# Early passes, new orders at both ends, and multiplications of ones, in a four-layer graph kernel on one core

## The chip, the core and the metric

The kernel runs on one core of a Trainium2 chip. The metric is the device time of one execution in microseconds (us). A core has TensorE (PE, matmuls into the accumulation memory PSUM), VectorE (DVE), ScalarE (ACT), GpSimd (POOL) and SyncE (SP, which here issues all DMAs). Each runs its own instructions in order and waits on semaphores.

## The reference

x is 128 graphs of 128 nodes with 256 features, adj 128 matrices of 128 x 128. Four graph layers follow each other, each with a residual and a layer norm:

```
x = _layernorm(x + _L0_gnn_ref(x, adj, ...))   # hypergraph conv 256->512, relu, norm, conv 512->256, + x
x = _layernorm(x + _L1_gnn_ref(x, adj, W))     # relu([x, (adj @ x) / deg] @ W.T)
x = _layernorm(x + _L2_gnn_ref(x, adj, ...))   # three times adj @ (x @ W) + b, relu behind the first two
x = _layernorm(x + _L3_gnn_ref(x, adj, ker))   # relu((adj @ x) @ ker) * (row of x is not all zero)
```

In layer 0 the incidence matrix is H = (adj != 0), used as D^-1 H B^-1 H^T.

## The kernel before

**Work.** Two graphs at a time make a pair; there are 64 pairs. For each pair TensorE works through 18 groups of matmuls, named by stage: G, Tr, Gx, R (in two halves), P (two halves and the sums of squares, psum<-ones,sq), GP for layer 0; xT, XAB, AXB for layer 1; Ax2, H1, H1W, H2, H2W, AP3 for layer 2; Ax3, TK for layer 3. Most products are made from a high and a low part of each operand (X_hi rounded to fp32r, X_lo = X - X_hi): hi x hi, hi x lo, lo x hi. `product` issues these three for each term, behind a wait for the high and the low part of the data. Gx, Ax2, H2 and Ax3 are plain fp32 products with the state as the stationary side, and psum<-A_f,x is both Ax2 and Ax3.

**Between the groups.** ScalarE takes a result out of PSUM and rounds it (`high_...`, `round_...`), VectorE or GpSimd makes the low part (`low_...`). A norm (n1 to n4) goes: sum, `stats`, `mean_var` (together `moments`) on VectorE, `root` on ScalarE, `invert` and `shift` on VectorE, and the scaling on ScalarE (`make_x2`, `make_x3`, `make_x4`; in the profile ACT x L961). `make_x3` gives the x that Ax3 multiplies.

**Order.** Each engine has `fill()`, `body(n)` for n from 7 to 61, and `drain()`, written out as lists of calls. In `body` pairs n to n-5 are in flight at once, one stage each. Which PSUM bank (0 to 7) a stage writes is in BANK, and for the pairs of fill and drain in BANK_OF; a wait on TensorE keeps a stage from writing a bank that is still read:

```
def bank(stage, pair):
    return BANK_OF.get((stage, pair), BANK[stage])
def make_x3(p):
    if begun(p - 1):
        act.wait_ge(pe_did["Ax3"], upto(p - 1))
        act.wait_ge(n4.summed, upto(p - 1))
        act.wait_ge(x3_nz, upto(p - 1))
    apply(n3, p, x3)
```

`upto(p)` is the semaphore's value when pair p has passed. `copy_GT(p)` and `round_GT(p)` read the transposes of Tr(p) from their bank, bank 0 in the loop. `wide_var`, `root_h` and `make_p` make the norm inside layer 0; `root_h` is ACT h_std in the profile. In the fill `w2_columns` (psum<-w2g,ones) and `betaW_rows` (psum<-n_s,beta_b) are two sums over the weights.

Of the kernel before, what the change touches and what calls it, by code (L numbers as in the profile page):

```python
# [16 lines left out]
BANK = dict(R0=1, R1=0, Ax2=0, Tr=0, GP=4, H1=1, Gx=1, XAB=2, AXB=2, TK=2, H2=3, xT=4, P=4,  # L17
# [30 lines left out]
def build(nc, x, adjT, w1T, w2T, wab, v1, v2, v3, wk, columns, rows, eye, out):  # L48
# [5 lines left out]
    with ExitStack() as ctx:  # L54
# [23 lines left out]
        eps_c, wait_pad = sb("eps_c", [1]), sb("wait_pad", [1])  # L78
# [46 lines left out]
        class Norm:  # L125
            def __init__(self, name, sums=True, lag=0, moments=None):
                if sums:
                    self.s = sb(f"{name}_s", [2, D])
                self.st, self.lag = sb(f"{name}_st", [2, 6]), lag
# [160 lines left out]
        def _(sp):  # L290
# [37 lines left out]
            def fill():  # L328
                load_at(0)
                sp.dma_start(columns_s[:], columns).then_inc(columns_loaded, 16)  # L330
                load_at(1)
                load_w2(1)
                load_w2(0)
                load_at(2)
                load_w1(0)
                load_x(0)
                load_v(2)
                load_w1(1)
                sp.dma_start(ident[:], eye).then_inc(eye_loaded, 16)
                load_v(0)  # L340
                load_wab(0)
                load_x(2)
                load_at(3)
                load_v(3)
                load_v(1)
                load_x(1)
                sp.dma_start(rows_b[:], rows.partition_broadcast(C)).then_inc(rows_loaded, 16)
# [1951 lines left out]
```

## Time and profile before

| | before |
|---|---|
| median of 3 runs | 1405.96 us (1405.39 to 1407.59) |
| the profiled execution | 1406.28 us, span 1404.5 us |
| TensorE busy | 1378.7 us, 98% of the span, 10896 matmul records |
| VectorE, ScalarE, GpSimd busy | 1135.4, 1126.3, 1013.2 us |
| granted TensorE clock, mean | 0.995 |
| read and written | 28.12 and 16.78 MB |

The span runs from the first to the last instruction that the profile shows; the time has 1.78 us more around it. In a row of the timeline the first number is the start in us from the span's beginning, the second the length from the first start to the last end of the xN records in it.
### The profile page before, as it was taken

Reading aid. Unit: us, or ns where it says so; the run is one execution under the profiler, and the core shown is the slowest. Engines: PE = TensorE matmul, PEld = TensorE weight load, DVE = VectorE, ACT = ScalarE, POOL = GpSimd, SP = SyncE. Lnnn points to the kernel's source line nnn. Section 1 sums busy time; section 2 is a strip of 40 time slices with the busy share of each in tenths; the row PEclk is TensorE's granted clock in tenths of the full one; section 3 lists DMA queues with packets and bytes.
Section 4 is the critical chain, followed back from the end, with each engine's and each line's share of the span. In section 5 each row is a group of like instructions: output and inputs, shape, how many; then the busy total and the mean of one; then the engine's idle time right before and its main releaser. Section 6 shows DMA issues by size and latency. Waiting matters only on the chain. (4 is left out here: it accounts for less than half of the span.)

```text
span 1404.5 us, 35429 instructions
## 1 busy us (share of the span) xinstructions
PE 1378.7 (98%) x10896; PEld 1336.8 (95%) x10896; DVE 1135.4 (81%) x4086; ACT 1126.3 (80%) x2639; POOL 1013.2 (72%) x1065
## 2 busy tenths in 40 slices
PE   7999999999999999999999999999999999999995
PEld 7999999999999999999999999999999999999995
DVE  7888888787887887787887888877878877878886
ACT  6777887887887878878878878778878788788775
POOL 5857778777777787787787787777777877877530
PEclk9999999999999999999999999999999999999998
DMA  4100110101101101101101101011011011010001
GB/s 141 35 21 20 39 36 24 39 30 30 39 20 39 39 21 39 39 20 39 39 20 39 38 21 39 28 32 39 20 39 39 20 39 39 20 39 28 1 16 38
DMA packets 29961, 47.17 MB, mean 34 GB/s; under 512 B 3408, under 2 KB 12240, under 8 KB 29776
## 3 DMA queue, kind: packets, MB, share of 16 engines
q1 hardware_dynamic: 29776, 44.91, 10.1%
q8 instruction: 90, 1.47, 0.4%
q14 instruction: 95, 0.78, 0.2%
HBM read 28.12 MB, written 16.78 MB: 32 GB/s over the span
## 5 line engine op out<-in xcount | busy, mean ns | idle before, releaser
L961 ACT ACTIVATE x<-n_s,n_shift,n_rstd 128x256 f32<-128x256 f32 x384 | 208.4, 591 | 6.5 <-DVE n_shift L1550 5.1
L216 POOL TENSOR_TENSOR r_lo<-r_f,r_hi 128x512 fp32r<-128x512 f32 x122 | 157.7, 1293 | 45.3 <-ACT r_hi L942 40.1
L209 POOL TENSOR_TENSOR h_lo<-h_f,h_hi 128x512 fp32r<-128x512 f32 x122 | 158.1, 1296 | 40.3 <-ACT h_hi L942 40.1
L2111 POOL TENSOR_TENSOR n_s<-tk,mask 128x512 f32<-128x512 f32 x60 | 62.5, 1042 | 141.8 <-DVE mask L1603 135.1
L375 PE MATMUL psum<-v_hi,h_hi 128*128 128x256 f32 x512 | 149.6, 292 | 1.2 <-ACT tk L1123 1.0
L375 PE MATMUL psum<-w2c_hi,r_hi 128*128 128x258 f32 x512 | 145.8, 285 | 0.2 <-issue 0.2
L375 PE MATMUL psum<-w2c_lo,r_hi 128*128 128x258 f32 x512 | 144.5, 282 | 0.0
L375 PE MATMUL psum<-v_hi,h_lo 128*128 128x256 f32 x512 | 144.4, 282 | 0.0
L375 PE MATMUL psum<-gx_hi,w1T_hi 128*128 128x256 f32 x512 | 144.3, 282 | 0.1
L375 PE MATMUL psum<-v_lo,h_hi 128*128 128x256 f32 x512 | 144.1, 282 | 0.0
L1526 DVE BATCH_NORM_STATS2 n_st<-n_s 128x6 f32<-128x256 f32 x384 | 142.1, 412 | 2.2
L375 PE MATMUL psum<-gx_lo,w1T_hi 128*128 128x256 f32 x512 | 143.8, 281 | 0.0
L375 PE MATMUL psum<-gx_hi,w1T_lo 128*128 128x256 f32 x512 | 143.8, 281 | 0.0
L375 PE MATMUL psum<-w2c_hi,r_lo 128*128 128x258 f32 x512 | 143.8, 281 | 0.0
L375 PE MATMUL psum<-A_f,x 128*128 128x128 f32 x1024 | 136.2, 276 | 6.5 <-ACT x L961 6.1
L966 ACT ACTIVATE h_f<-psum,columns 128x256 f32<-128x256 f32 x256 | 107.6, 471 | 34.9 <-PE psum L375 34.6
L375 PEld LDWEIGHTS psum<-A_f,x 128*128 128x128 f32 x1024 | 125.5, 192 | 7.9 <-issue 7.8
L956 ACT ACTIVATE n_std<-psum,eps_c 128x2 f32<-128x2 f32 x165 | 42.3, 257 | 93.6 <-DVE psum L1535 93.6
L209 POOL TENSOR_TENSOR p_lo<-p_f,p_hi 128x512 fp32r<-128x512 f32 x61 | 78.1, 1280 | 51.5 <-ACT p_hi L942 51.5
L209 DVE TENSOR_TENSOR ax_lo<-psum,ax_hi 128x512 fp32r<-128x512 f32 x128 | 88.4, 691 | 26.8 <-ACT ax_hi L942 23.3
L375 PE MATMUL psum<-wab_hi,x1T_hi 128*128 128x512 f32 x256 | 106.5, 416 | 0.0
L966 ACT ACTIVATE r_f<-psum,columns 128x256 f32<-128x256 f32 x256 | 100.5, 468 | 2.2 <-PE psum L375 2.1
(166 smaller groups left out, 5379.8 us busy)
## 6 DMA issues: line engine op xcount, KB each, us to landing
x_in<-x_in_dram SPq DMA_DIRECT2D x64, 256.0 KB, 2.8
out<-x SPq DMA_DIRECT2D x64, 256.0 KB, 2.0
at_in<-adjT SPq DMA_DIRECT2D x64, 128.0 KB, 2.2
x<-v_in SPq DMA_DIRECT2D x3, 256.0 KB, 5.6
n_s<-w2T_in SPq DMA_DIRECT2D x2, 256.0 KB, 3.5
r_f<-w1T_in SPq DMA_DIRECT2D x2, 256.0 KB, 5.5
h_f<-wab_in SPq DMA_DIRECT2D x2, 256.0 KB, 5.9
tk<-wk_in SPq DMA_DIRECT2D x1, 256.0 KB, 5.5
```

Of the source, the lines that this page charges most:

```text
L209: return e.tensor_tensor(dst[1][:], src, f(dst[0][:]), ALU.subtract).then_inc(signal, 1)
L216: e.tensor_tensor(r_s[1][:, half], r_f[:, half], f(r_s[0][:, half]), ALU.subtract).then_inc(r_lo[h], 1)
L375: return pe.matmul(o, a, b, start=start, stop=stop)
L956: act.activation(nm.std[:], nm.mv(p)[:, :, 1], ACT.Sqrt, bias=eps_c[:, 0:1]).then_inc(nm.rooted, 1)
L961: last = act.activation(dst[:, g, :], nm.s[:, g, :], ACT.Identity, scale=nm.rstd[:, g:g + 1], bias=nm.shift[:, g:g + 1])
L966: return act.activation(dst[:, m].rearrange("p g c -> p (g c)"), psum[:, bank(stage, p), (m % 2) * 2 * C:(m % 2 + 1) * 2 * C], ACT.Relu, b ...
L1526: last = dve.bn_stats(nm.st[:, g, :], sum_in_psum(p, g) if nm is n1 else nm.s[:, g, :])
L2111: pool.tensor_tensor(n4.s[:], tk[:], bc(mask[:], [C, 2, D], 2), ALU.mult).then_inc(tk_masked, 1)
```

## The change

All products but Gx, Ax2, H2 and Ax3 are issued in two parts: `early`, the matmuls that need only the high part of the data, and `late`, behind the wait for its low part. H2 moves from bank 3 to bank 0. The orders of fill and drain are new on all engines, with a new BANK_OF and a new order of the first loads. Each norm has its own pad for the memset between stats and mean_var. TensorE multiplies ones by ones ten times before all else, twelve times ahead of Ax3(63) and three times ahead of TK(63), the last two groups of the program; nothing reads these results. In `body` the calls keep their order on TensorE, with some waits changed, on VectorE, and on SyncE; on ScalarE and GpSimd GT's steps move up.

```diff
-BANK = dict(R0=1, R1=0, Ax2=0, Tr=0, GP=4, H1=1, Gx=1, XAB=2, AXB=2, TK=2, H2=3, xT=4, P=4,
+BANK = dict(R0=1, R1=0, Ax2=0, Tr=0, GP=4, H1=1, Gx=1, XAB=2, AXB=2, TK=2, H2=0, xT=4, P=4,
...
-            def product(o, terms, start=True, stop=True):
-                for t, (a, b) in enumerate(terms):
+            def early(o, terms, state, start=True):
+                for t, ab in enumerate(terms):
+                    a, b = ab
                     mm(o, a[0], b[0], start and t == 0, False)
-                    mm(o, a[0], b[1], False, False)
-                    last = mm(o, a[1], b[0], False, stop and t == len(terms) - 1)
+                    mm(o, a[1 - state], b[state], False, False)
+
+            def late(o, terms, state, stop=True):
+                for t, ab in enumerate(terms):
+                    a, b = ab
+                    last = mm(o, a[state], b[1 - state], False, stop and t == len(terms) - 1)
                 return last
...
             def TK(p):
                 if p == 0:
                     pe.wait_ge(v_lo, 4)
+                outs = by_state("TK", p, ax3, wk_s)
                 pe.wait_ge(ax3_hi, upto(p))
-                pe.wait_ge(ax3_lo, upto(p))
-                weigh("TK", p, ax3, wk_s)
+                for j, (o, terms) in enumerate(outs):
+                    early(o, terms, 1)
+                    if j == 0:
+                        pe.wait_ge(ax3_lo, upto(p))
+                    last = late(o, terms, 1)
+                last.then_inc(pe_did["TK"], 1)
...
+            def keep_busy(b, times):
+                for _ in range(times):
+                    mm(psum[:, b, 0:C], ones[:], ones[:], True, True)
+
             def fill():
+                pe.wait_ge(consts_step, 1)
+                keep_busy(BANKS - 1, 10)
                 G(0)
...
             def body(n):
+                pe.wait_ge(gx_lo, n)
                 R(n - 1, 0)
-                pe.wait_ge(gt_hi, n)
+                pe.wait_ge(h2_relu, n - 3)
                 R(n - 1, 1)
...
                 Gx(n)
-                pe.wait_ge(n2.summed, n - 1)
+                pe.wait_ge(gt_hi, n + 1)
                 H2(n - 3)
...
             def drain():
+                pe.wait_ge(p_made, 61)
+                R(61, 0)
+                pe.wait_ge(ax3_lo, 58)
                 pe.wait_ge(h1w_out, 59)
                 pe.wait_ge(n2.shifted, 60)
-                pe.wait_ge(p_made, 61)
                 G(62)
...
+                keep_busy(bank("Ax3", 63), 12)
+                Ax3(63)
                 pe.wait_ge(h1w_out, 64)
-                TK(62)
-                pe.wait_ge(ax3_lo, 62)
-                Ax3(63)
-                pe.wait_ge(n3.summed, 63)
+                keep_busy(bank("TK", 63), 3)
                 TK(63)
...
             def mean_var(nm, p):
                 dve.wait_ge(nm.stats, upto(p))
-                dve.memset(wait_pad[:], 0.0)
+                dve.memset(nm.pad[:], 0.0)
```

Three places of the new order, as the built programs have it.

TensorE at the very end, before: TK(62), then Ax3(63) (psum<-A3_f,x3) and TK(63), each TK made of wk and the two parts of ax3.

```order
L375 MATMUL psum<-wk_lo,ax3_hi 128x256
L375 MATMUL psum<-wk_hi,ax3_lo 128x256
L375 MATMUL psum<-A3_f,x3 128x128 x4
L375 MATMUL psum<-wk_hi,ax3_hi 128x256
L375 MATMUL psum<-wk_lo,ax3_hi 128x256
L375 MATMUL psum<-wk_hi,ax3_lo 128x256
```

The same place now:

```order
L374 MATMUL psum<-wk_lo,ax3_hi 128x256
L374 MATMUL psum<-wk_hi,ax3_lo 128x256 x2
L374 MATMUL psum<-ones 128x128 x12
L374 MATMUL psum<-A3_f,x3 128x128 x4
L374 MATMUL psum<-ones 128x128 x3
L374 MATMUL psum<-wk_hi,ax3_hi 128x256
L374 MATMUL psum<-wk_lo,ax3_hi 128x256
L374 MATMUL psum<-wk_hi,ax3_hi 128x256
L374 MATMUL psum<-wk_lo,ax3_hi 128x256
L374 MATMUL psum<-wk_hi,ax3_lo 128x256 x2
```

In each half of TK the four matmuls with ax3_hi now stand ahead of the two with ax3_lo, and the ones stand ahead of either group.

ScalarE in one pass of the loop, from square_mean (h_mean2) to high_gx, before: x3 is make_x3, GT1 and GT1_hi are copy_GT and round_GT.

```order
L1042 ACTIVATE h_mean2<-psum 128x2
L1046 ACTIVATE h_std<-h_veps 128x2
L961 ACTIVATE x3<-n3_s,n3_shift,n3_rstd 128x256 x2
L942 ACTIVATE p_hi<-p_f 128x512
L942 ACTIVATE GT1<-psum 128x256
L942 ACTIVATE h1w<-psum 128x512
L942 ACTIVATE ax3_hi<-psum 128x512
L942 ACTIVATE GT1_hi<-psum 128x256
L942 ACTIVATE gx_hi<-psum 128x512
```

And now:

```order
L1091 ACTIVATE h_mean2<-psum 128x2
L991 ACTIVATE GT1<-psum 128x256
L1095 ACTIVATE h_std<-h_veps 128x2
L991 ACTIVATE GT1_hi<-psum 128x256
L1010 ACTIVATE x3<-n3_s,n3_shift,n3_rstd 128x256 x2
L991 ACTIVATE p_hi<-p_f 128x512
L991 ACTIVATE h1w<-psum 128x512
L991 ACTIVATE ax3_hi<-psum 128x512
L991 ACTIVATE gx_hi<-psum 128x512
```

Both copies of GT have moved ahead of x3.

VectorE in the fill, between sum_n3(2) and make_p(5), before: n3 is the norm of pair 2, n4 that of pair 1, and h_veps is written by wide_var(5).

```order
L1711 TENSOR_TENSOR n3_s<-psum,x2c0 128x512
L1526 BN_STATS n3_st<-n3_s 128x6 x2
...
L1535 BN_AGGR n3_mv<-n3_st 128x2 x2
L1546 RECIPROCAL n3_rstd<-n3_std 128x2
L1550 SCALAR_TENSOR_TENSOR n3_shift<-n3_mv,n3_rstd 128x2
L1526 BN_STATS n4_st<-n4_s 128x6 x2
...
L1535 BN_AGGR n4_mv<-n4_st 128x2 x2
L1546 RECIPROCAL n4_rstd<-n4_std 128x2
L1550 SCALAR_TENSOR_TENSOR n4_shift<-n4_mv,n4_rstd 128x2
L1650 SCALAR_TENSOR_TENSOR psum<-psum,h_mean2 128x2
L1653 SCALAR_TENSOR_TENSOR h_veps<-psum,eps_c 128x2
```

And now:

```order
L1760 TENSOR_TENSOR n3_s<-psum,x2c0 128x512
L1575 BN_STATS n3_st<-n3_s 128x6 x2
L1580 MEMSET n3_pad 128x1
L1584 BN_AGGR n3_mv<-n3_st 128x2 x2
L1575 BN_STATS n4_st<-n4_s 128x6 x2
L1595 RECIPROCAL n3_rstd<-n3_std 128x2
L1580 MEMSET n4_pad 128x1
L1584 BN_AGGR n4_mv<-n4_st 128x2 x2
L1599 SCALAR_TENSOR_TENSOR n3_shift<-n3_mv,n3_rstd 128x2
L1595 RECIPROCAL n4_rstd<-n4_std 128x2
L1599 SCALAR_TENSOR_TENSOR n4_shift<-n4_mv,n4_rstd 128x2
...
L1702 SCALAR_TENSOR_TENSOR h_veps<-psum,eps_c 128x2
```

The statistics of n4 now stand between those of n3 and the inverse of n3's root, and n3's shift behind them.

## Rows read from the trace of the kernel before

**Rows 1.** Windows: stretch, then busy us and records by engine, clock, DMA share, GB/s.

```profile
200.00:1250.00 1050.00, 1049.89 (x8375) 1022.57 (x8374) 851.25 (x3101) 860.70 (x2019) 802.31 (x838) 1.00 0.10 32
```

**Rows 2.** Timeline of TensorE, sums of squares of two neighbouring pairs in the loop.

```profile
604.31 0.50 PE L375 MATMUL psum<-ones,sq 128*128 128x1 f32 x4
...
625.62 0.50 PE L375 MATMUL psum<-ones,sq 128*128 128x1 f32 x4
```

**Rows 3.** Waits: who waited for whom, us in total, times, longest.

```profile
PE psum L375 <- ACT x L961: 6.1, 5, 3.2
```

**Rows 4.** Timeline of TensorE in the first 16 us.

```profile
6.14 0.80 PE L375 MATMUL psum<-BH,HT 128*128 128x258 f32 x2 [6.14 <-POOL BH L2089]
7.72 3.78 PE L375 MATMUL psum<-w2g,ones 128*128 128x256 f32 x8 [0.78 <-DVE w2g L1718]
11.31 0.69 PE L415 MATMUL psum<-ident,Gd 128*128 128x128 f32 x2
...
13.66 1.89 PE L375 MATMUL psum<-n_s,beta_b 128*128 128x256 f32 x8
```

**Rows 5.** Timeline of VectorE and ScalarE in the first 16 us.

```profile
0.83 0.17 DVE L1754 MEMSET ones<- 128x128 f32 x1 [0.83 <-PEq L2291]
...
10.21 0.61 DVE L1625 SCALAR_TENSOR_TENSOR Gd<-psum,dinv,Gl 128x128 f32<-128x128 f32 x2
...
12.25 0.36 ACT L942 ACTIVATE GT<-psum 128x256 f32<-128x256 f32 x1
12.52 0.61 ACT L942 ACTIVATE v_hi<-x 128x512 fp32r<-128x512 f32 x1
...
14.49 0.69 DVE L209 TENSOR_TENSOR gx_lo<-psum,gx_hi 128x512 fp32r<-128x512 f32 x1 [0.42 <-ACT gx_hi L942]
```

**Rows 6.** Timeline around Ax3(2), ScalarE and TensorE.

```profile
114.94 0.20 ACT L1046 ACTIVATE h_std<-h_veps 128x2 f32<-128x2 f32 x1 [1.62 <-DVE h_veps L1653]
115.09 1.09 ACT L961 ACTIVATE x<-n_s,n_shift,n_rstd 128x256 f32<-128x256 f32 x2
...
116.32 1.13 PE L375 MATMUL psum<-A_f,x 128*128 128x128 f32 x8 [1.24 <-ACT x L961]
```

**Rows 7.** Timeline of one pass: Tr and Ax3 on TensorE, root_h and make_x3 on ScalarE.

```profile
604.67 0.41 PE L415 MATMUL psum<-ident,Gd 128*128 128x128 f32 x2
...
607.09 1.05 PE L375 MATMUL psum<-A_f,x 128*128 128x128 f32 x8
...
605.45 0.20 ACT L1046 ACTIVATE h_std<-h_veps 128x2 f32<-128x2 f32 x1 [0.43 <-DVE h_veps L1653]
605.59 1.10 ACT L961 ACTIVATE x<-n_s,n_shift,n_rstd 128x256 f32<-128x256 f32 x2
```

**Rows 8.** Timeline at the start of the drain, VectorE and TensorE.

```profile
1295.02 0.16 DVE L1550 SCALAR_TENSOR_TENSOR n_shift<-psum,n_rstd 128x2 f32<-128x2 f32 x1
...
1295.28 0.48 PE L375 MATMUL psum<-BH,HT 128*128 128x258 f32 x2 [0.83 <-issue]
```

**Rows 9.** Timeline of TensorE: last of H1(63), first of H1W(63).

```profile
1372.24 0.28 PE L375 MATMUL psum<-ax_hi,v_lo 128*128 128x256 f32 x1
...
1375.86 0.36 PE L375 MATMUL psum<-v_hi,h_hi 128*128 128x256 f32 x1
```

**Rows 10.** The chain that ended last: start, us, what; pairs 62 and 63.

```profile
1383.80 1.14 PE psum L375 x8
...
1386.43 1.65 PE psum L375 x12
...
1391.30 1.74 PE psum L375 x8
...
1393.68 0.70 DVE ax_lo L209
...
1394.52 2.91 PE psum L375 x12
```

**Rows 11.** Windows at the end, columns as in rows 1.

```profile
1392.00:1393.00 1.00, 1.00 (x5) 0.72 (x4) 0.00 (x0) 0.00 (x0) 0.00 (x0) 0.50 0.00 0
```

More of the change, by code:

```diff
@@ L425, in R @@
                     pe.wait_ge(w1_lo, h + 1)
+                outs = [(psum[:, bank(f"R{h}", p), (m % 2) * 2 * C:(m % 2 + 1) * 2 * C],
+                         [(part(w1T_s, ALL, kk, cols(m)), part(gx, ALL, kk)) for kk in range(KD)])
+                        for m in (2 * h, 2 * h + 1)]
                 pe.wait_ge(gx_hi, upto(p))
-                pe.wait_ge(gx_lo, upto(p))
-                for m in (2 * h, 2 * h + 1):
-                    last = product(psum[:, bank(f"R{h}", p), (m % 2) * 2 * C:(m % 2 + 1) * 2 * C],
-                                   [(part(w1T_s, ALL, kk, cols(m)), part(gx, ALL, kk)) for kk in range(KD)])
+                for j, (o, terms) in enumerate(outs):
+                    early(o, terms, 0)
+                    if j == 0:
+                        pe.wait_ge(gx_lo, upto(p))
+                    last = late(o, terms, 0)
                 last.then_inc(pe_did[f"R{h}"], 1)
@@ L435, in P @@
                     pe.wait_ge(w2c_lo, 1)
+                outs = [(psum[:, bank("P", p) + g, 0:D + 2],
+                         [(part(r_s, ALL, m, g), part(w2c_s, ALL, m)) for m in (2 * h, 2 * h + 1)]) for g in range(2)]
+                pe.wait_ge(r_hi[h], upto(p))
+                for o, terms in outs:
+                    early(o, terms, 1, start=h == 0)
                 pe.wait_ge(r_lo[h], upto(p))
-                for g in range(2):
-                    product(psum[:, bank("P", p) + g, 0:D + 2],
-                            [(part(r_s, ALL, m, g), part(w2c_s, ALL, m)) for m in (2 * h, 2 * h + 1)],
-                            start=h == 0, stop=h == 1)
+                for o, terms in outs:
+                    late(o, terms, 1, stop=h == 1)
             def squares(p):
@@ L448, in GP @@
             def GP(p):
+                outs = [(psum[:, bank("GP", p), g * D:(g + 1) * D],
+                         [(part(GT_s[p % 2], ALL, g), part(p_s, ALL, g))]) for g in range(2)]
                 pe.wait_ge(p_hi, upto(p))
-                pe.wait_ge(p_lo, upto(p))
                 pe.wait_ge(gt_lo, upto(p))
-                for g in range(2):
-                    last = product(psum[:, bank("GP", p), g * D:(g + 1) * D],
-                                   [(part(GT_s[p % 2], ALL, g), part(p_s, ALL, g))])
+                for j, (o, terms) in enumerate(outs):
+                    early(o, terms, 0)
+                    if j == 0:
+                        pe.wait_ge(p_lo, upto(p))
+                    last = late(o, terms, 0)
                 last.then_inc(pe_did["GP"], 1)
@@ L502, in H1W @@
                     pe.wait_ge(v_lo, 2)
+                outs = by_state("H1W", p, h1_s, v_s[1])
                 pe.wait_ge(h1_hi, upto(p))
-                pe.wait_ge(h1_lo, upto(p))
-                weigh("H1W", p, h1_s, v_s[1])
+                for j, (o, terms) in enumerate(outs):
+                    early(o, terms, 1)
+                    if j == 0:
+                        pe.wait_ge(h1_lo, upto(p))
+                    last = late(o, terms, 1)
+                last.then_inc(pe_did["H1W"], 1)
             def H2(p):
@@ L862, in drain @@
+                xT(62)
+                squares(63)
+                pe.wait_ge(h1w_out, 61)
+                H2W(60)
+                pe.wait_ge(n1.done, 63)
+                H1(61)
+                pe.wait_ge(ax2_lo, 62)
+                pe.wait_ge(h2_relu, 61)
+                XAB(62)
                 pe.wait_ge(p_made, 64)
                 GP(63)
-                pe.wait_ge(tk_relu, 59)
-                XAB(62)
-                pe.wait_ge(h1w_out, 61)
-                H2W(60)
-                pe.wait_ge(n2.summed, 62)
@@ L1433, in drain @@
-                root_h(63)
+                relu_h1(60)
+                round_h1(60)
+                make_x4(57)
+                relu_tk(58)
+                round_r(63, 1)
+                copy_A(62)
+                root(n1, 62)
+                root(n2, 61)
+                root(n3, 59)
                 copy_h1w(60)
-                round_p(63)
-                high_x1T(62)
-                relu_tk(58)
+                make_x2(61)
+                make_x3(59)
                 relu_h2(60)
@@ L1994, in drain @@
+                shift(n3, 59)
+                make_x1(62)
+                stats(n4, 58)
+                mean_var(n4, 58)
+                low_h2(dve, 60)
+                low_ax2(61)
+                wide_var(63)
+                count_nonzero(59)
+                invert(n4, 58)
+                shift(n4, 58)
+                make_p(63)
+                low_A(dve, 62)
                 low_x1T(62)
-                moments(n2, 61)
+                low_h2w(60)
+                low_p(dve, 63)
+                low_ax3(59)
@@ L2065, in _ @@
+                invert(n4, 63)
+                shift(n4, 63)
             fill()
```

1157 lines of the change are left out of this document (606 added, 551 removed), and 39 rows, old and new, of the table BANK_OF.

## The prediction

> **What bounds the kernel now.** I read the page first: in its 40 slices TensorE is at 9 tenths everywhere but in the first and the last. A table of windows then says how full the middle is: from 200 to 1250 us it is busy 1049.89 of 1050 us, at the granted clock of 1.00 [rows 1]. The timeline gives the pass: the sums of squares of two neighbouring pairs start 21.31 us apart [rows 2]. So 55 passes make 1172 us that no wait lengthens, and a better beginning or end can only win back what those two hold: the span of 1404.5 us less 64 x 21.31 = 1363.8 us is some 41 us, of which under 4 are the two weight sums of the beginning (1.89 us for one at full speed, below). The list of waits names the largest holes: TensorE waited for x from ScalarE 6.1 us in 5 waits, the longest 3.2 [rows 3].
>
> The profiled execution took 1406.28 us, 1.78 more than its span and 0.3 more than the median of the three runs, 1405.96. I make the sum against 1406.28 and take 0.3 off at the end.
>
> **The beginning, first 20 us.** TensorE's first matmul starts at 6.14 us, when BH is ready, and the kernel after waits there for the same chain. Behind it the eight w2g records take 3.78 us; the eight beta_b records, of the same form, take 1.89 us six microseconds later [rows 4]. The clock field says 1.00 for both, but by their lengths the first run at the 1.2 GHz level and the second at 2.4; what TensorE did before them is nothing and two matmuls, or steady work. The ten matmuls of ones (20 records, a 128 x 128 one costing at the low level half of a w2g record, 0.22 us, so 4.4 us) start when VectorE has written ones at 1.0 us and end at 5.5, ahead of 6.14: they delay nothing, and cover most of the idle time. If they lift the clock, the w2g sum ends at 9.4 instead of 11.3.
>
> The Trainium skill (TensorE: Matmul & The Clock Gate, "What's actually happening") says that the half rate is the default and that activity releases it. By that rule, the trace agrees, and the ones would give all 1.9 us. I don't take them all, since TensorE isn't the last to arrive. The transposes at 11.31 need Gd, written until 10.82; with VectorE's low_A(0) gone it can be there some 0.4 us sooner. R(0, 0), behind the beta_b sum, needs gx_lo, which runs from 14.49 to 15.18 [rows 4, 5]. In the new order spread_beta's four instructions stand between the scaling of G and gx_lo, and w2's low half, which P(0, 0) needs, is made after one more scaling of G. So I count P(0, 0) nearly where it was, and 0.5 us won by the early passes of R and P: a low part of 0.69 us now stands beside four or eight matmuls of 0.12 (the twelve of a TK take 1.65, below). Bounds: 0 and 1.9.
>
> **The rest of the fill.** The one large hole is ahead of Ax3(2): 1.24 us idle, 1.4 late by the starts. h_std there starts at 114.94 and x right behind it at 115.09, and h_std waited 1.62 us for VectorE's h_veps [rows 6]: VectorE stood in order through moments and invert_shift of n3 and n4, each time waiting for a root. The new fill has the loop's own order there (the VectorE piece of the order shown above), in which the same wait for h_veps doesn't hold x up [rows 7]. I take 1.2 us of it, and 0.3 of the smaller waits (bounds 0 and 1.5: they can go or be replaced). Fill: 0.5 + 1.2 + 0.3 = 2.0 us.
>
> **The loop.** Order of groups, matmuls and records stay. An early pass costs nothing in the loop, since nothing waits there, and gains nothing. What moves is on ScalarE: both copies of GT now stand ahead of make_x3, because H2 in bank 0 has to wait for round_GT. The transposes end at 604.67 + 0.41 = 605.08, so copy_GT can start at 605.11; the next instruction follows a 0.36 us copy after 0.27 us (12.25 to 12.52, [rows 5]), at 605.38, and root_h isn't ready before 605.45 anyway. round_GT comes 0.09 to 0.14 behind it and x another 0.27 later: 605.81 to 605.86 instead of 605.59. x takes 1.10, so it is done at 606.91 to 606.96. Ax3 starts at 607.09 and needs x about 0.14 before, which is what passes between x and Ax3(2) at 116.32 (115.09 + 1.09 + 0.14) [rows 6, 7]. So 0.26 us of slack shrink to about 0.02. I count 0.01 us a pass, 0.5 us in all. Bounds: 0, and no overlap at all on ScalarE (605.11 + 0.38 + 0.20 + 0.38 + 1.09 + 0.14 = 607.30, or 0.21 late in each of 55 passes, 11.6 us).
>
> **The drain, step by step.** (1) G(62) now comes after R(61, 0). It started at 1295.28 after 0.83 us idle (1.0 by the starts, since matmuls of 0.28 follow each other in 0.12), behind n_shift of n2, which starts at 1295.02 [rows 8]; a half of R (12 x 0.12 = 1.4 us) covers that: 1.0 us won. (2) Ax3(61) stands ahead of H1(63) instead of behind: 0.9 lost. (3) Between the last matmul of H1(63) at 1372.24 and H1W(63) at 1375.86 lie 3.5 us, with H2W(62), Ax3(61) and its wait [rows 9]; now H2W(62) and TK(61), 24 x 0.12 = 2.9 us, and H1W(63) starts on h1_hi: 0.6 won. (4) In the chain TensorE runs pair 62 (Ax3 1.14, TK 1.65) at the full clock and pair 63 (1.74 and 2.91) at 0.50 [rows 10, 11]. If the ones keep the clock, Ax3(63) wins 0.6 and TK(63) 1.26: 1.9 us. Eight records of a 128 x 128 product take 1.05 us [rows 7], so the 24 of the first twelve ones take some 3.0 in a hole of 3.2 [rows 3], and the six of the last three 0.8 in the stretch of high and low: they delay nothing. (5) TK(63) starts its first four matmuls on ax3_hi: from the end of high it takes 0.70 for the low part, 0.16 between and 1.65 = 2.5 us at full clock; now the low part is done at 0.8 and 8 matmuls are left (1.1 with the tail), 1.9. But make_x4(62), whose shift now waits behind low_ax3(63), ends at about 2.0, ahead of relu_tk(63): 0.5 won. TK(62) and the sum ahead of x3(63) win 0.2 the same way. The store and last norm behind TK(63) stay at 7.1. Drain: 1.0 - 0.9 + 0.6 + 1.9 + 0.5 + 0.2 = 3.3. Waits earlier in the drain I take as equal; bounds 2 us less and 1 more.
>
> Sum: 2.0 - 0.5 + 3.3 = 4.8 us; 1406.28 - 4.8 - 0.3 = 1401.2 us.
>
> **Rivals.**
> A. The above: 1401.2, its own range 1398.5 to 1403.1. Chance 0.56.
> B. **make_x3 comes too late in every pass.** ScalarE is in order, so all that is put ahead of x delays it; with no overlap 0.21 us a pass, 1401.2 - 0.5 + 11.6 = 1412.3 us. It decides from 0.15 us a pass on, where 8 us eat the gain and leave 0.2% loss; at 0.05 it costs 2.8 and hides the gain. For it: a margin of 0.02 us. Against: the rows of copies that start 0.27 apart. Chance 0.12, 0.05 of it slower. The Trainium skill (TensorE: Matmul & The Clock Gate, "Architectural detail") calls ScalarE's queue strictly first in, first out, which speaks against putting two copies ahead of x; the trace agrees (x stood behind a late h_std until 115.09).
> C. **The ones don't hold the clock.** The granted clock is 0.50 at 1392 us, the 1.2 GHz level, behind 3.2 us without a matmul [rows 3, 11]. If the ones don't keep it up, 1.9 us are missing: 1403.1. Chance 0.08. Against it: other waits for x, shorter and with work between them, left the clock at 1.00.
> D. **The written-out orders bring new waits.** The last pair's P, GP and XAB come later in the drain than before by 2 to 7 us of work, and H2W(63) stands right behind H2(63) with no TK(61) between. If 2 to 3 us of waits come back, 1403.1 to 1404.5. Chance 0.16.
> E. More of the holes close (the start's full 1.9 and all 1.5 of the fill are 2.6 more, and the drain's bound 1 more): 1398.6 and less. Chance 0.08.
>
> **How the numbers follow.** 0.2% is 2.8 us, about what a measurement of this kernel can tell from no change. Faster (below 1403.1): A, E, most of C, 0.03 of B, 0.04 of D: 0.76. Slower (above 1408.8): 0.06. Same: 0.18. The range leaves out most of E and the worst of B and D: 1398.0 to 1404.8.
>
> **What would show it.** w2g's eight records at 1.9 us instead of 3.78 with the ones ahead; the wait before Ax3(2) below 0.3; no wait at the start of the drain; the passes at 21.31 to 21.33, and x ending 0.13 to 0.18 before Ax3; the last TK at 1.65 us with clock 1.00. A pass of 21.4 or more, or over 3 us of new waits between 16 and 120 or 1295 and 1370 us, makes it wrong.

## The result, and the profile after

The changed kernel takes 1394.36 us (median of 4 runs, 1393.31 to 1394.52) beside 1405.68 us (4 runs, 1405.36 to 1407.59) for the kernel before on the same chip: a ratio of 0.9915, 95% interval 0.9898 to 0.9932. That is 11.3 us, where I had forecast 4.8 and a time of 1401.2, and it lies outside my range of 1398.0 to 1404.8. The profiled execution took 1393.31 us with a span of 1391.2, 1.05 us less than the median. The kernel ran a second time later (`a_again` below): median 1394.40, profiled span 1392.3.

The spans of the two profiled executions, 1404.5 and 1391.2, differ by 13.3 us, 2.0 more than the medians: the one before took 0.6 more than its median, the one after 1.05 less, and the time outside of the span is 2.15 us and not 1.78. It is 2.1 to 2.2 in every profile with the new fill and drain and 1.8 in every one with the old; whether it lies ahead of the span or behind it the profiles don't show. So the gains by part below, read from spans, add up to more than 11.3.

The page's part 1 after: busy time, share of the span, instructions.

```profile
PE 1376.9 (99%) x10946; PEld 1335.9 (96%) x10946; DVE 1134.6 (82%) x4092; ACT 1122.7 (81%) x2639; POOL 1003.6 (72%) x1059
```

TensorE's busy time is nearly what it was, with 50 more records of ones in it. Windows, columns as in [rows 1], of the kernel before:

```profile
60.00:120.00 60.00, 58.49 (x456) 56.10 (x455) 50.43 (x174) 43.48 (x104) 38.63 (x42) 1.00 0.06 19
```

and of the kernel after:

```profile
60.00:120.00 60.00, 60.00 (x475) 58.04 (x474) 52.84 (x180) 47.97 (x112) 36.63 (x38) 1.00 0.08 24
...
200.00:1250.00 1050.00, 1049.98 (x8410) 1022.04 (x8409) 855.59 (x3114) 863.25 (x2031) 800.53 (x838) 1.00 0.11 33
```

The two lines from 60 to 120 us say that the holes of the fill are gone there, the one ahead of Ax3(2) [rows 6] among them. The line from 200 us on hides what I had missed: TensorE is as full as in [rows 1], but 8410 records fit in where 8375 did. A busy share near 1 says that no matmul waits, not how closely one follows the other. To see that, I take the sums of squares of pairs 6 and 60, which are 54 passes apart. Timelines of TensorE, before:

```profile
135.08 0.50 PE L375 MATMUL psum<-ones,sq 128*128 128x1 f32 x4
...
1286.66 0.50 PE L375 MATMUL psum<-ones,sq 128*128 128x1 f32 x4
```

and after:

```profile
131.07 0.50 PE L374 MATMUL psum<-ones,sq 128*128 128x1 f32 x4
...
1277.59 0.50 PE L374 MATMUL psum<-ones,sq 128*128 128x1 f32 x4
```

They cut the kernel in three:

| us | before | after | second run | gain | forecast |
|---|---|---|---|---|---|
| start to pair 6 | 135.1 | 131.1 | 131.0 | 4.0 | 2.0 |
| 54 passes | 1151.6 | 1146.5 | 1146.2 | 5.1 to 5.4 | -0.5 |
| pair 60 to the end | 117.8 | 113.6 | 115.0 | 4.3, 2.9 | 3.3 |

A pass takes (1286.66 - 135.08) / 54 = 21.326 us before and 21.232 after: 0.094 us less, which I had put at nothing. The other two parts came out 2.0 better and between 0.4 worse and 1.0 better than forecast.

**The start.** Timeline of TensorE after, columns as in [rows 4]:

```profile
1.06 4.26 PE L374 MATMUL psum<-ones 128*128 128x128 f32 x20 [1.06 <-DVE eps_c L1804]
5.89 0.50 PE L374 MATMUL psum<-BH,HT 128*128 128x258 f32 x2 [0.57 <-POOL BH L2207]
7.82 3.45 PE L374 MATMUL psum<-w2g,ones 128*128 128x256 f32 x8 [1.42 <-DVE w2g L1767]
```

The ones end ahead of G(0), as drawn up, but w2g takes 3.45 us and not 1.9. The windows give a granted clock of 0.60 from 8 to 9 us and 0.50 from 9 to 11, the 1.2 GHz level: in this execution the 4.26 us of ones did not leave the clock up behind 1.42 us of waiting. A little later a wait shows that the kernel before did not have; it is ahead of P(0, 0), for w2's low half:

```profile
20.15 0.36 PE L374 MATMUL psum<-w2c_hi,r_hi 128*128 128x258 f32 x1 [0.83 <-DVE w2c_lo L1785]
```

**The end.** The last groups of TensorE after:

```profile
1368.90 1.13 PE L374 MATMUL psum<-A_f,h1w 128*128 128x128 f32 x8
...
1371.75 0.36 PE L374 MATMUL psum<-v_hi,h_hi 128*128 128x256 f32 x1 [1.72 <-ACT h_hi L991]
...
1377.00 2.84 PE L374 MATMUL psum<-ones 128*128 128x128 f32 x24
...
1380.29 1.16 PE L374 MATMUL psum<-A_f,x 128*128 128x128 f32 x8 [0.46 <-ACT x L1010]
1381.29 0.83 PE L374 MATMUL psum<-ones 128*128 128x128 f32 x6
```

and the chain that ended last, from TK(63) on:

```profile
1382.14 1.95 PE psum L374 x12
1384.09 0.02 issue
1384.11 0.02 ACT tk L1172
```

Ax3(63) takes 1.16 us instead of 1.74 and TK(63) 1.95 instead of 2.91 [rows 10], with the ones filling the hole ahead. In the second line a new wait shows: H2W(63) stands right behind H2(63) and waits for high_h2, 1.72 us idle and 1.97 late by the starts. It is the longest wait of TensorE after the first 10 us. My rival D had named that place.

### The profile page after: what moved, and what is told of

Read it like the earlier page. It is cut to its first block, busy times and chain, and to the rows that moved or that the text cites. A ratio compares the mean times of both kernels' runs of the same rounds, so it can differ in the third digit from the quotient of the medians.

```text
span 1391.2 us, 35333 instructions
## 1 busy us (share of the span) xinstructions
PE 1376.9 (99%) x10946; PEld 1335.9 (96%) x10946; DVE 1134.6 (82%) x4092; ACT 1122.7 (81%) x2639; POOL 1003.6 (72%) x1059
## 4 chain that ended last, share of the span: by engine, by line
PE 98%; ACT 1%; issue 0%; DVE 0%; DMA 0%; SPq 0%; ACTq 0%; DVEq 0%
PE psum L374 95%; PE psum L473 2%; PE psum L417 1%; DMA n_s<-w2T_in 0%; ACT x L1010 0%; ACT tk L1172 0%; ACT h_hi L991 0%; DVE w2c_lo L1785 0%; DVE w2g L1767 0%; ACT w2c_hi L991 0%; ACT r_f L1015 0%; SPq L291 0%; ACT h_f L1015 0%; DVE n_st L1575 0%; DVE n_s L260 0%
## 5 line engine op out<-in xcount | busy, mean ns | idle before, releaser
L374 PE MATMUL psum<-v_hi,h_hi 128*128 128x256 f32 x512 | 137.8, 292 | 2.0 <-ACT h_hi L991 2.0
L374 PE MATMUL psum<-v_lo,h_hi 128*128 128x256 f32 x512 | 133.3, 282 | 0.0
L374 PE MATMUL psum<-gx_hi,w1T_hi 128*128 128x256 f32 x512 | 132.3, 281 | 0.0
L374 PE MATMUL psum<-gx_hi,w1T_lo 128*128 128x256 f32 x512 | 131.9, 281 | 0.0
L374 PE MATMUL psum<-w2c_hi,r_hi 128*128 128x258 f32 x512 | 129.5, 284 | 0.8 <-DVE w2c_lo L1785 0.8
L374 PE MATMUL psum<-w2c_lo,r_hi 128*128 128x258 f32 x512 | 129.4, 283 | 0.0
L374 PE MATMUL psum<-v_hi,h_lo 128*128 128x256 f32 x512 | 102.1, 281 | 0.0
L374 PE MATMUL psum<-gx_lo,w1T_hi 128*128 128x256 f32 x512 | 101.8, 281 | 0.0
L374 PE MATMUL psum<-wab_lo,x1T_hi 128*128 128x512 f32 x256 | 100.9, 394 | 0.0
L208 DVE TENSOR_TENSOR x1T_lo<-psum,x1T_hi 128x512 fp32r<-128x512 f32 x64 | 44.2, 691 | 69.3 <-ACT x1T_hi L991 69.3
```

The lines of the kernel that those rows point to most:

```text
L208: return e.tensor_tensor(dst[1][:], src, f(dst[0][:]), ALU.subtract).then_inc(signal, 1)
L374: return pe.matmul(o, a, b, start=start, stop=stop)
```

## The experiments

A pass in each table and sentence is worked out as above, from pair 6's and pair 60's sums of squares. "R 2.73" is the time from R's first matmul to the next group, from neighbouring starts, the value that most passes have.

### Is it the order of matmuls, or the early copies of GT?

`b_order` gives the kernel before the new order of matmuls with all waits ahead of the group; `b_gt` gives it the new order of ScalarE and GpSimd in body:

```diff
                 square_mean(n - 1)
+                copy_GT(n)
                 root_h(n - 1)
+                round_GT(n)
                 make_x3(n - 4)
                 round_p(n - 1)
-                copy_GT(n)
                 copy_h1w(n - 3)
                 high_ax3(n - 4)
-                round_GT(n)
```

`a_old_product` is the changed kernel with `product` and its waits as before, and `a_no_ones` is the changed kernel without the three calls of `keep_busy`.

> The kernel before, in which each product issues its matmuls in the order of the changed kernel (those on the high part first), with both waits still ahead of the group: no matmul starts earlier on a high part, and nothing else differs. In the changed kernel a pass of the loop is 0.094 us shorter (21.326 to 21.232), which my prediction had put at nothing. Theory O (a part of that is the order itself: by stage, AXB, R, H2W, H1 and GP are 0.010 to 0.017 us shorter and P 0.029 longer): a pass of 21.28 us, some 2 to 3 us less in all, near 1403.2, with Gx still 0.94 long. Theory S (what counts is that a group starts on its high part alone, and the matmuls themselves cost the same in any order): a pass of 21.32 to 21.33 and 1405.7. My own step in the prediction (order and early passes gain nothing in the loop) goes with S.

> The kernel before with the body's calls of ScalarE and GpSimd as the changed kernel has them: both copies of GT ahead of make_x3, and low_GT ahead of low_p. Nothing else differs. Half of what a pass lost lies in Gx: the time from its first record to the second is 0.161 us before and 0.112 after, and copy_GT, for which Gx waits, starts 3.02 us behind the sums of squares before and about 0.9 after, with Gx at 3.67. Theory G (GT comes so late before that TensorE can't issue Gx ahead, although the trace shows no wait): Gx at 0.89 and a pass of 21.27, some 3 us less in all, near 1402.9. Theory K (it is H2's bank or its wait, since Gx lies right ahead of H2): Gx stays at 0.94 and the pass at 21.32, 1405.7. If my rival B were true after all, the pass would be above 21.33.

> The changed kernel with the products of the kernel before: hi x hi, hi x lo, lo x hi for each term, behind the waits for both parts. All orders, banks and ones stay. Theories O and G together: a pass of 21.27 (Gx at 0.89, the rest as before), 2.5 us lost in the loop, and some 1 us more in fill and drain where a group started on its high part: 1397.5 to 1398.5. Theory S: 5 us lost in the loop, 1399.5 or more. If early passes matter nowhere, 1394.4.

> The changed kernel without any of the three sets of ones. I had priced the ones at the end at 1.9 us and those at the start as a part of 0.5 (bounds 0 to 1.9). From the trace of the changed kernel the first matmuls behind the ones at the start still run at the low level (w2g's records are 0.43 us apart), so I expect nothing from the start, and 1.9 us from the end: Ax3(63) 1.7 and TK(63) 2.9 us long, 1396.3. Rival: the last groups keep the clock in the new order without ones, since the hole ahead of Ax3(63) may be shorter now: 1394.4.

| | median us | pass | pair 6 at | behind pair 60 |
|---|---|---|---|---|
| b_order | 1404.87 | 21.316 | 134.4 | 118.2 |
| b_gt | 1404.46 | 21.292 | 134.6 | 118.0 |
| a_old_product | 1404.73 | 21.150 | 137.6 | 122.8 |
| a_no_ones | 1394.72 | 21.227 | 130.3 | 115.4 |

(Before beside them: 1405.74.) The order of matmuls gave 0.010 us a pass, not 0.045, and the median, 0.9 us lower (ratio 0.9995, 0.9986 to 1.0005), can't be told from no change. The copies of GT gave 0.034: Gx starts at the same place of the pass, but H2 follows it 0.049 sooner, of which H2 itself gives 0.023 back (0.812 to 0.836 on average). Before, copy_GT ended 0.29 us ahead of Gx and Gx took 0.94 us:

```profile
607.33 0.36 ACT L942 ACTIVATE GT<-psum 128x256 f32<-128x256 f32 x1
...
607.98 1.10 PE L375 MATMUL psum<-GT,x_in 128*128 128x128 f32 x8
...
608.92 1.06 PE L375 MATMUL psum<-A_f,h1w 128*128 128x128 f32 x8
```

and in b_gt, where copy_GT starts 2.85 us ahead of Gx and ends 2.47 ahead, 0.90:

```profile
603.99 0.38 ACT L942 ACTIVATE GT<-psum 128x256 f32<-128x256 f32 x1
...
606.84 1.06 PE L375 MATMUL psum<-GT,x_in 128*128 128x128 f32 x8
...
607.74 1.08 PE L375 MATMUL psum<-A_f,h1w 128*128 128x128 f32 x8
```

No view calls these 0.05 us a wait; they lie between Gx's first and second record. Theory G holds for Gx, with 1404.46 us where it had 1402.9. The pass didn't grow with make_x3 behind both copies, so rival B doesn't hold.

`a_old_product` was the surprise, twice. Its passes are shorter than those of the changed kernel, 21.150, so that early and late cost 0.08 us a pass there; and it is as slow as the kernel before, since both ends fall apart: 6.5 us up to pair 6 and 9.2 behind pair 60 (7.8 beside `a_again`, in which, as here, the clock fell at H2W(63)). TensorE's largest waits in it are for low parts, and in the changed kernel no wait of TensorE for x1T_lo, h_lo, ax_lo or r_lo is in the list (who waited for whom, us in total, times, longest):

```profile
PE psum L374 <- DVE x1T_lo L208: 3.5, 5, 1.1
PE psum L374 <- DVE h_lo L208: 3.4, 2, 2.4
PE psum L374 <- DVE ax_lo L208: 3.3, 5, 1.1
PE psum L374 <- DVE r_lo L215: 1.4, 1, 1.4
```

### What are the ones worth, and can both ends and loop have their best?

`a_again` is the changed kernel. `a_no_start` leaves out the ten ones, `a_no_end` the twelve and the three. `c_mix` calls the products of the kernel before in body alone:

```diff
             def body(n):
-                R(n - 1, 0)
+                R_whole(n - 1, 0)
...
-                TK(n - 4)
+                TK_whole(n - 4)
```

> The changed kernel once more, unchanged, as the kernel that the next three are read against. Theory L (when w2g is done depends on when the load of w2T_in lands, which differs from run to run): the w2g sum starts somewhere between 6.8 and 7.9 us, and its records are 0.43 or 0.22 us apart. Median 1394.4.

> The changed kernel without the ten ones at the start; those at the end stay. Without all the ones the median was 1394.72 against 1394.36, and the time from pair 60's sums of squares to the end of the span 115.4 against 113.6. If the ones at the start gain nothing: 1394.4 and 113.6 behind pair 60. If they cost (the run without them was 0.8 us ahead by pair 6): 1393.6. If they gain what my bound allowed: up to 1396.3.

> The changed kernel without the twelve and the three ones ahead of Ax3(63) and TK(63). My step (4) says 1.9 us: the time from pair 60's sums of squares to the end is 115.4 instead of 113.6, Ax3(63) 1.7 us long, TK(63) 1.0 longer, and the median 1396.3. If the two sets of ones trade places (start costs, end gains), 1396.3 as well, and a_no_start 1393.6. If neither counts: 1394.4 in both.

> The changed kernel, in whose body the products are those of the kernel before (hi x hi, hi x lo, lo x hi, behind both waits); fill and drain keep early and late. With the old product everywhere a pass was 21.150 us (21.232 in the changed kernel), R 2.731 against 2.823, while fill lost 6.5 us and from pair 60 to the end 9.2. Theory E (early passes gain where groups follow their data closely, at both ends alone, and cost 0.08 us a pass in the loop): 54 passes x 0.082 = 4.4 us less, pass 21.15, 1390.0. Rival: R's short form comes from something in fill that the old product sets, such as the alignment of the instructions, and not from the loop's own code: pass 21.23, 1394.4.

| | median us (range) | pass | behind pair 60 |
|---|---|---|---|
| a_again | 1394.40 (1394.36 to 1394.61) | 21.226 | 115.0 |
| a_no_start | 1393.60 (1392.78 to 1394.18) | 21.230 | 113.6 |
| a_no_end | 1395.18 (1394.02 to 1395.83) | 21.232 | 115.8 |
| c_mix | 1389.05 (1388.79 to 1390.22) | 21.155 | 113.5 |

**The ones at the start gain nothing.** Without them w2g takes 3.78 us in all four profiles of the new orders. With them it takes 3.11 to 3.76 in six profiles and 1.99 in three (a_old_product, and r_whole and tk_whole below). The place of its start doesn't tell them apart: the short ones start at 7.23 to 7.59 us, the long ones at 7.06 to 7.82. Where it is short, TensorE stands behind it for Gd; in a_old_product 0.91 us:

```profile
7.23 1.99 PE L374 MATMUL psum<-w2g,ones 128*128 128x256 f32 x8 [0.74 <-DVE w2g L1724]
10.14 0.41 PE L414 MATMUL psum<-ident,Gd 128*128 128x128 f32 x2 [0.91 <-DVE Gd L1631]
```

The Trainium skill (TensorE: Matmul & The Clock Gate, "What's actually happening") also says that the same kernel differs from run to run in how many matmuls it starts at the low level. The trace agrees: the same ones preceded 3.45 and 1.99 us. It gains nothing further on: pair 0's sums of squares start at 24.04 and 24.34 us in r_whole and tk_whole, and at 24.03 to 24.64 in the profiles with the long w2g and the same orders. The median without them is 0.8 us lower than a_again's, with no overlap of the four times each.

**Those at the end are worth 0.8 to 1.9 us in the profiles.** Without them 115.4 (a_no_ones) against 113.6, as step (4) says. But a_again, with them, has 115.0, and a_no_end 115.8. In the medians they are worth 0.8 (a_no_end to a_again), and all three sets together 0.4 (1394.72 to 1394.36), which is less than four runs can tell from nothing. A window behind the hole ahead of H2W(63) in the changed kernel's first profile:

```profile
1372.00:1374.00 2.00, 2.00 (x18) 1.87 (x18) 1.42 (x9) 1.10 (x3) 0.00 (x0) 1.00 0.00 0
```

and in a_again:

```profile
1372.00:1374.00 2.00, 2.00 (x12) 1.94 (x11) 1.10 (x9) 0.50 (x2) 0.00 (x0) 0.60 0.00 0
1374.00:1376.00 2.00, 2.00 (x12) 2.00 (x12) 0.69 (x1) 0.89 (x2) 0.00 (x0) 0.55 0.00 0
```

In a_again and in a_no_end (and in r_whole and r_ahead below) the clock fell to the 1.2 GHz level 0.3 to 1.6 us behind the hole ahead of H2W(63); in the first profile of the changed kernel, a_no_start, a_no_ones, c_mix, p_mix and tk_whole, with the same hole, it stayed at 1.00. So in some executions the clock is lost at a hole ahead of the ones. In a_no_end, where that had happened, the clock was up again for Ax3(63) in spite of 3.26 us of waiting, and only TK(63) ran at 0.50; in a_no_ones both did. That is why leaving the ones out costs 0.8 in one pair of profiles and 1.9 in the other.

**c_mix** came at 1389.05: theory E holds, a pass is 21.155 and both ends stay.

### Where R's short form comes from

In a_old_product and c_mix R takes 2.731 us, in the changed kernel 2.823, in the kernel before 2.837. `r_whole` gives body the old R alone, `r_ahead` keeps its new order but waits ahead, `b_h2` is b_gt with H2 in bank 0 in the loop and TensorE's new waits in body:

```diff
             def body(n):
+                pe.wait_ge(gx_lo, n)
                 R(n - 1, 0)
-                pe.wait_ge(gt_hi, n)
+                pe.wait_ge(h2_relu, n - 3)
                 R(n - 1, 1)
...
                 Gx(n)
-                pe.wait_ge(n2.summed, n - 1)
+                pe.wait_ge(gt_hi, n + 1)
                 H2(n - 3)
```

`best1` is c_mix without the first ones and with ones in the new hole:

```diff
                 H2(63)
                 pe.wait_ge(h2_relu, 63)
+                keep_busy(bank("H2W", 63), 8)
```

> The changed kernel, with the old R alone in body (hi x hi, hi x lo, lo x hi, behind both waits); all other products keep early and late. In the kernel with all old products in body a pass is 21.155 us and R 2.731, in the changed kernel 21.227 to 21.232 and 2.823. Theory R1 (R's short form comes from R's own order or waits): R 2.73, pass 21.14, since P and H1W keep their forms of the changed kernel, 1389.5. Theory R2 (it comes from what TensorE did before R, as TK's order): R 2.82, 1394.4.

> The changed kernel, in whose body R keeps the order of early and late but waits for both parts ahead of its first matmul. If a wait in the middle of the group breaks R's short form: R 2.73 and some 5 us less, 1389.5. If the order does: 2.82 and 1394.4. In b_order, where the waits stood ahead too, R was 2.842.

> The kernel before with all that the changed kernel's body has on TensorE, ScalarE and GpSimd but the products: H2 in bank 0, its wait for gt_hi instead of n2.summed, the waits for gx_lo ahead of R and for h2_relu between its halves, and the early copies of GT. Fill and drain stay. b_gt, which has the copies alone, had a pass of 21.292. Theory W (bank and waits of the body shorten groups: H2W by 0.015, H1 0.010, AXB 0.011, R 0.106 in the kernel that has them with the old product): pass 21.15, 1396.5. Rival (those come from what is outside of the body, such as the place of buffers in memory, since each norm has its own pad now): 21.29, 1404.4.

> c_mix (old products in body, early and late in fill and drain, median 1389.05) without the ones at the start and with eight ones ahead of H2W(63), where TensorE waits 1.97 us. In two of four runs of the changed kernel or of one without some ones (the second run of the changed kernel, and the one without the ones at the end) the granted clock fell to 0.50 for some 3 us right behind that wait, with 1.4 us lost in H2W(63), Ax3(62) and AP3(63); in the others it stayed at 1.00. Theory H (that hole is where the clock falls, depending on where the execution stands, and ones in it keep it): 113.6 us from pair 60's sums of squares to the end in every run, some 0.5 to 1 us less in the median, and 0.4 to 0.8 less for the ones at the start: 1388.0. Rival: the ones change nothing there, and those at the start did no harm: 1389.0.

r_whole: 1392.92, pass 21.228, R 2.823. r_ahead: 1393.46, 21.227, R 2.823 (the passes are those of the changed kernel; the medians are 1.5 and 0.9 us below a_again's, which stays unexplained). b_h2: 1403.71, 21.278, R 2.837. best1: 1388.80 (1388.71 to 1389.02), 21.154, 113.5 behind pair 60. Neither R's order nor its waits give the short form, nor does body as a whole: theory W fell, and b_h2 adds only 0.014 us to b_gt. What was left was outside of body: fill and drain, or the place of the buffers. best1's eight ones fill the hole and its four times lie within 0.3 us, but the median is only 0.25 below c_mix, less than I can tell from nothing; that they keep the clock is likely and not shown.

### The place of the buffers

The kernel before has a one-element buffer `wait_pad` between `eps_c` and `x_in`; the changed kernel has it no more (each norm has its own, allocated behind all operands of the loop's matmuls). So what lies behind it, gx_hi and gx_lo among them, sits 32 bytes lower, while the weights, allocated ahead of it, stay. In the change as told ahead of the prediction it is the line about each norm's pad. `p_before` changes nothing else in the kernel before:

```diff
-        eps_c, wait_pad = sb("eps_c", [1]), sb("wait_pad", [1])
+        eps_c = sb("eps_c", [1])
...
         n3, n4 = Norm("n3", lag=4, moments=BANK["AP3"]), Norm("n4", lag=5, moments=BANK["H1"])
+        wait_pad = sb("wait_pad", [1])
```

`p_bh2` is the same in b_h2, and `p_mix` puts a one-element buffer back into c_mix. `tk_whole` has the old GP and TK in body.

> The kernel before, with its one-element buffer wait_pad allocated behind all other buffers instead of between eps_c and x_in, so that every buffer from x_in on lies where the changed kernel has it. No instruction changes. Theory M (the place of the operands in memory sets how closely matmuls follow each other): R falls from 2.837 to 2.73 or 2.82, H2W from 1.523 to 1.506, H1 from 1.429 to 1.419, a pass is 0.05 to 0.14 us shorter, and the time 1398 to 1403. Rival N (those came from the instructions around them): 21.326 and 1405.6.

> b_h2 (the changed kernel's body but for its products: 21.278 a pass) with wait_pad allocated last in the same way. Theory M: H2W 1.506, H1 1.419, R 2.731, and a pass of 21.15, as in the changed kernel with old products, so 1403.7 - 54 x 0.127 = 1396.8. Rival N: 21.278 and 1403.7.

> c_mix (1389.05, pass 21.155) with a one-element buffer nobody uses between eps_c and x_in, so that all buffers behind lie where the kernel before had them. Theory M: R back at 2.837, H2W 1.523, H1 1.429, a pass of 21.28 and 1389.05 + 54 x 0.12 = 1395.6. Rival N: 1389.05.

> The changed kernel, in whose body GP and TK, the two groups ahead of R, alone are the old products. With R alone old, R stayed at 2.823. If R's length depends on how the groups ahead of it run into it: R 2.731, pass 21.14, 1389.5. If it needs all products old: R 2.823, 1394.4.

| | median us | pass | R | H2W | H1 |
|---|---|---|---|---|---|
| before (beside these) | 1405.72 | 21.326 | 2.837 | 1.523 | 1.429 |
| p_before | 1398.59 | 21.201 | 2.731 | 1.508 | 1.419 |
| p_bh2 | 1396.06 | 21.153 | 2.731 | 1.508 | 1.419 |
| p_mix | 1396.95 | 21.276 | 2.838 | 1.522 | 1.429 |
| tk_whole | 1393.28 | 21.230 | 2.823 | 1.506 | 1.419 |

Theory M holds in all three: **moving a one-element buffer, which the program writes and no result needs, is worth 7.1 us** (ratio 0.9947, 0.9932 to 0.9962). In p_mix a buffer that nothing touches, at the old place, takes it away again. R in the kernel before, from its first matmul to G:

```profile
611.94 0.28 PE L375 MATMUL psum<-gx_hi,w1T_hi 128*128 128x256 f32 x1
...
614.42 0.28 PE L375 MATMUL psum<-gx_hi,w1T_hi 128*128 128x256 f32 x1
...
614.78 0.40 PE L375 MATMUL psum<-BH,HT 128*128 128x258 f32 x2
```

and in p_before:

```profile
608.28 0.28 PE L376 MATMUL psum<-gx_hi,w1T_hi 128*128 128x256 f32 x1
...
610.66 0.28 PE L376 MATMUL psum<-gx_hi,w1T_hi 128*128 128x256 f32 x1
...
611.01 0.40 PE L376 MATMUL psum<-BH,HT 128*128 128x258 f32 x2
```

2.84 and 2.73 us for the same 24 matmuls: 0.118 and 0.114 from one to the next, and a record's length, 0.28, shows none of it. Not all groups gain: of the 0.125 us of a pass R gives 0.095, H2W, AXB and H1 0.010 to 0.015 each, and H1W becomes 0.011 longer (averages over 54 passes). tk_whole leaves R at 2.823.

The last two ask what it is in the place. `p_64` adds a second one-element buffer to the kernel before; `best2` puts every buffer of best1 at a multiple of 64 bytes, and the rows of w2c and xbw too (n is the number of elements of a buffer's row):

```diff
         def sb(name, shape, dt=F32):
...
+            if (n + 7) // 8 % 2:
+                ctx.enter_context(nc.sbuf_tensor(f"{name}_gap", [C, 1], F32))
...
-        w1T_s, w2c_s = hi_lo("w1T", [KD, DH]), hi_lo("w2c", [KH, D + 2])
+        w1T_s, w2c_s = hi_lo("w1T", [KD, DH]), hi_lo("w2c", [KH, D + 16])
```

> best1 (1388.8, pass 21.154), with every buffer at a multiple of 64 bytes (a 32-byte gap behind each of odd length) and the rows of w2c and xbw 272 elements apart instead of 258, so that theirs start at multiples of 64 too. Theory 64, extended to the stationary and the moving side alike: P (2.880) and AXB (0.809) shorten as R did, by up to 4%, a pass of 21.03 to 21.10 and 1382 to 1386. If only the buffers that theory M moved count, 21.15 and 1388.8. If closer spacing brings new waits: above.

p_64: 1402.39 us beside 1406.03, pass 21.264, R 2.856, H2W 1.496, XAB 2.858 (2.890 before). So 32 bytes up is a gain too, of half the size, but R is longer than ever: the rule of 64 fell. best2: 1385.59 us (1385.36 to 1385.83), pass 21.105; the time is inside the expected range. Averages over 54 passes, beside best1: H1W 1.394 instead of 1.445, H2W 1.481 instead of 1.507, TK 1.402 instead of 1.415, but R 2.759 instead of 2.739, and P and AXB, for which I had changed the rows of w2c and xbw, 2.887 and 0.814 instead of 2.880 and 0.809. It is the fastest of all, 0.9857 of the kernel before (0.9841 to 0.9874), and the gain is not where I had put it.

## Why the prediction was wrong

**The step that failed** is the loop: "Order of groups, matmuls and records stay. An early pass costs nothing in the loop, since nothing waits there, and gains nothing." With "I count 0.01 us a pass, 0.5 us in all" for make_x3 the term was -0.5; it measured +5.1. Its first sentence isn't wholly true of the change either: inside each product the order of matmuls is new, as the diff shows. What stood in its place, in us a pass:

| part of the change | from | pass | in 54 |
|---|---|---|---|
| every buffer from x_in on 32 bytes lower | before to p_before | -0.125 | -6.7 |
| body: GT early, H2's bank, waits | p_before to p_bh2 | -0.048 | -2.6 |
| early and late in the products | c_mix to the changed kernel | +0.077 | +4.1 |
| sum | | -0.096 | -5.2 |

The measured difference is 0.094; the 0.002 between are p_bh2's pass, 21.153, and c_mix's, 21.155. I never asked what the diff does to the layout of memory, and treated 0.12 us from matmul to matmul as a constant. The first and the third term lie within that constant's rounding, 0.114 to 0.118; the second is the gap inside Gx. The first and the third also meet in one group: the place takes 0.095 us from R and early and late put 0.081 back (and 0.022 on P), so that R in the changed kernel is only 0.018 shorter than before. Early and late at the old place were not run. There the order of the matmuls alone, with all waits ahead, gave 0.010 (b_order).

**Rival B** (make_x3 late) is out: x ends about 0.2 us later in the pass, and Ax3 starts where it did, 2.77 us behind the sums of squares instead of 2.78. The margin, forecast at 0.02 us, was thin enough that two passes show 0.2 us of waiting ahead of Ax3, as two did ahead of Gx before. I had looked at this move for its cost alone. Its other side, GT ready long before Gx, was worth 0.034 us a pass.

**The fill** gave 4.0 us instead of 2.0. The step on Ax3(2) was right: its wait is gone, 1.2 to 1.4 us. "0.3 of the smaller waits" was mis-sized: those of 0.56, 0.35, 0.32 and 0.27 us between 50 and 90 us went as well, 1.5 in all, which was my bound. The first pair's sums of squares came 0.25 us sooner (24.73 to 24.48), where I had 0.5 with P(0, 0) nearly in its place; the new wait of 0.83 us for w2's low half stands ahead of it. Of the 0.85 that are left of the 4.0, the six passes up to pair 6 give some 0.56 if each is 0.094 shorter, as in the loop (an estimate).

**The ones at the start.** "If they lift the clock, the w2g sum ends at 9.4": it ended at 11.3, and the sum was short in three of nine profiles. My reason for not counting all 1.9 us, that TensorE isn't the last to arrive, held: with w2g at the full clock it waited for Gd.

**The drain** gave 4.3 us instead of 3.3, or 2.9 in the executions that lose the clock ahead of Ax3(62). Step (1): no wait at its start any more, right. (3): 2.95 us from H1(63)'s last matmul to H1W(63) instead of 3.62, 0.7 for 0.6. (4): 1.9 shown by a_no_ones' profile, right for an execution that keeps the clock up to there; in the median the ones bring only 0.8 (a_no_end), since in some executions the clock falls at the hole ahead of H2W(63) instead. So the last groups keep the clock by the ones, and rival C doesn't hold there. (5): relu_tk(63) follows the end of high_ax3(63) after 2.02 us, forecast 2.0, and the tail behind it takes 7.1, as forecast. "Waits earlier in the drain I take as equal" was mis-sized by 1.0: of holes over 0.15 us between step (1)'s place and Ax3(63)'s, 4.7 us stood there before and 3.7 after, the 1.97 ahead of H2W(63) among them. That is the bound that I had given it, and the whole difference between 3.3 and 4.3.

Rival E, more of the holes closed, was the right direction with 1398.6 and less, but it had nothing of the loop in it.

**What the early passes are worth** I had seen at single places, 0.5 at the start and 0.5 at TK(63). For the new orders they are the ground: without them the same orders lose 6.5 us in the fill and 7.8 to 9.2 at the end, and stand behind the kernel before at both. The gain of an order and that of a finer wait can't be added up one by one here.

## What to carry to other kernels

When one engine is full, ask how closely its instructions follow each other, not only whether it waits: compare the time from one start to the next, group by group, over fifty passes. A diff that adds or removes a buffer moves all those behind it, and that alone was worth 7 us here, more than any step of the forecast; try a few layouts when the code stands still. Starting on the high part pays where data arrive just in time, at both ends, and in this layout cost time in the full loop: the two can be had in one program (c_mix), and the fastest version here, best2, is 20 us under the kernel before.

## What the runs showed of the hardware

The time from one fp32r matmul of 256 columns to the next changed with the place of the buffers: 0.114 or 0.118 us for R, with 32 bytes between the two layouts, and 32 bytes the other way 0.119. The Trainium skill (SBUF — State Buffer, "Operand start alignment") lets an operand start at any multiple of its element size and says of this that it is "about legality, not speed"; no run here bears on the first, and the four runs that move buffers alone (p_before, p_bh2, p_mix, p_64) show that speed does depend on the place, by 0.06 to 0.125 us a pass. No rule came out: XAB and H1W are shorter in the layout in which R is longest. R also has two lengths in one program: 2.731 us in most passes of a_old_product and c_mix and 2.823 in a few, and the other way round in the changed kernel, whose R turns to 2.731 in two of the fifty passes from pair 8 on. With R alone old, or GP and TK alone, it stays at 2.823. What tips it is open, and so is which of the moved buffers counts, and whether it is TensorE's own reads or their meeting with those of other engines and of DMAs, whose buffers moved too.

With the copy of GT ending 0.29 us ahead of Gx, Gx took 0.94 us, and with 2.5 us between (b_gt) 0.89, though no wait is shown in either.

The granted clock behind the hole ahead of H2W(63), 1.97 us by the starts, stayed at 1.00 in one execution of the changed kernel and fell to 0.50 for some 3 us in another. The Trainium skill (TensorE: Matmul & The Clock Gate, "What's actually happening") says that activity releases the half rate. The trace agrees in three profiles of nine, in which w2g behind the ten ones took 1.99 us; in the other six it took 3.11 to 3.76.
